# A row sum moved to VectorE, transposes made 32-bit, and three table loads moved behind a stage

## The reference, cut to what matters

```python
def reference(x, ...):                      # x: 8192 tokens x 4096 features, f32
    # layer 0a: LayerNorm, then up/gate projections, powers of |gate - point|, and a gated FFN
    a = attn_ref(layernorm(x))              # 4096 -> 1024 (x2), 7 x 1024 -> 4096, 4096 -> 9984 (x2) -> 4096
    x = x + layernorm(a)
    # layer 0b: LayerNorm, base projection plus a routed LoRA term
    xf = layernorm(x)
    base   = xf @ W_base.T + b_base         # 4096 -> 4096
    logits = xf @ W_router.T                # 8 experts, top 2
    h      = einsum('td,erd->ter', xf, A)   # 8 x 16 = 128 columns
    lora   = einsum('ter,te,eor->to', h, w, B) * 2
    return x + layernorm(base + lora)
```

## Time and profile before

| | us |
|---|---|
| timed runs | 6504.11 and 6038.73, median 6271.42 |
| the profiled execution | 6004.29 |
| its span, slowest core (core 5) | 6002.7 |
| its span, fastest core (core 3) | 5988.6 |

### The profile page before, as it was taken

One profiled execution on the slowest core, in us unless ns is written; L12 is line 12 of the kernel. 1 busy time (PEld: TensorE's weight loads), 2 busy tenths in 40 slices (PEclk: granted clock), 3 DMA queues, 4 the chain that ended last, 5 costly groups with the idle time before them and its releaser, 6 DMA issues.

```text
span 6002.7 us, 59549 instructions; the slowest of 8 cores (5988.6 to 6002.7 us)
## 1 busy us (share of the span) xinstructions
PE 5013.6 (84%) x23204; PEld 2279.0 (38%) x23204; DVE 942.9 (16%) x1384; ACT 486.2 (8%) x621; POOL 196.9 (3%) x371
## 2 busy tenths in 40 slices
PE   3887999999899999998999999799799800599940
PEld 2433444444344444443444444344344300244420
DVE  4551000011000000110000011011122233222221
ACT  3231000000000000000000000000000033100001
POOL 0000000000000000000000000000000000000000
PEclk9998999999999999999999999899899955799975
DMA  4344444445534334664343366666655733244445
GB/s 121 82 97 95 74 81 71 71 104 124 113 71 80 75 74 94 170 161 91 70 83 72 64 156 166 168 167 159 154 132 126 130 130 157 77 86 94 87 145 227
DMA packets 188163, 675.14 MB, mean 112 GB/s; under 512 B 21226, under 2 KB 86900, under 8 KB 154484
## 3 DMA queue, kind: packets, MB, share of 16 engines
q0 software_dynamic: 60784, 356.60, 33.7%
q1 hardware_dynamic: 127108, 314.73, 14.8%
HBM read 878.97 MB, written 148.90 MB: 171 GB/s over the span
## 4 chain that ended last, share of the span: by engine, by line
PE 77%; DMA 9%; DVE 7%; ACT 3%; issue 3%; SPq 1%; DVEq 0%; ACTq 0%; POOL 0%; POOLq 0%
PE P L222 74%; DMA xraw<-x_in 2%; DMA ft<-sc_f 2%; DMA W_glob<-w_fd_p 1%; ACT dt_sb L530 1%; DVE tmpr L543 1%; SPq L63 1%; PE S L239 1%; DVE tn L444 1%; DVE XL L453 1%; DMA BIG<-sc_tmp 1%; DMA W_glob<-w_fu_p 1%; DMA a1in<-sc_a1A 1%; DVE oring L1088 1%; DVE stc L813 1%
## 5 line engine op out<-in xcount | busy, mean ns | idle before, releaser
L222 PE MATMUL P<-XL,W_glob 128*128 128x512 bf16 x13056 | 2841.6, 380 | 110.6 <-DMA W_glob<-w_fu_p 42.7
L222 PE MATMUL P<-BIG,W_glob 128*128 128x512 bf16 x8576 | 1876.8, 381 | 114.5 <-DMA BIG<-sc_tmp 81.0
L222 PEld LDWEIGHTS P<-XL,W_glob 128*128 128x128 bf16 x13056 | 1274.7, 98 | 1663.9 <-issue 146.2
L222 PEld LDWEIGHTS P<-BIG,W_glob 128*128 128x128 bf16 x8576 | 835.5, 98 | 1142.0 <-issue 159.9
L599 DVE TENSOR_TENSOR BIG<-silu_sb,P 128x512 bf16<-128x512 f32 x156 | 107.3, 688 | 2105.0 <-PE P L222 2105.0
L594 ACT ACTIVATE silu_sb<-P 128x512 f32<-128x512 f32 x156 | 93.1, 597 | 2839.3 <-PE P L222 2839.3
L855 PE MATMUL P<-identb_sb,xlnb 128*128 128x128 bf16 x256 | 34.9, 304 | 294.3 <-DVE xlnb L843 285.2
L702 DVE TENSOR_TENSOR a_ring<-P,a1in 128x512 f32<-128x512 f32 x128 | 88.6, 692 | 778.3 <-PE P L222 346.3
L631 DVE TENSOR_TENSOR a1out<-P,a1in 128x512 f32<-128x512 f32 x128 | 88.6, 692 | 660.5 <-PE P L222 393.4
L713 ACT ACTIVATE sq<-a_ring 128x512 bf16<-128x512 f32 x64 | 40.4, 631 | 1314.0 <-DVE a_ring L702 1314.0
L855 PEld LDWEIGHTS P<-identb_sb,xlnb 128*128 128x128 bf16 x256 | 23.5, 132 | 305.6 <-issue 305.6
(11 more groups left out here) (124 smaller groups left out, 1213.9 us busy)
## 6 DMA issues: line engine op xcount, KB each, us to landing
W_glob<-w_fg_p POOLq DMA_DIRECT2D x78, 1024.0 KB, 9.5
W_glob<-w_fu_p POOLq DMA_DIRECT2D x78, 1024.0 KB, 13.9
W_glob<-w_fd_p POOLq DMA_DIRECT2D x96, 832.0 KB, 9.0
W_glob<-w_cat_p POOLq DMA_DIRECT2D x64, 896.0 KB, 9.1
xraw<-x_in SPq DMA_DIRECT2D x16, 2048.0 KB, 14.2
a1in<-sc_a1A SPq DMA_DIRECT2D x64, 512.0 KB, 8.3
W_glob<-w_b_p POOLq DMA_DIRECT2D x32, 1024.0 KB, 10.3
sc_a1A<-a1out SPq DMA_DIRECT2D x32, 512.0 KB, 2.7
```

The source lines that it names most:

```text
L222: inst = eng.matmul(out, l, r, start=(extra_first_start and i == 0), stop=(i == n - 1), skip_group_check=True)
```

## The change

The row sum of stage 1 moves from ScalarE to VectorE. In stage 6 xlnb6 becomes f32, and with it the transposes and their PSUM tile. The three tables are allocated after stage 6, and the first of their loads waits for the last VectorE and the last ScalarE operation of stage 6; the two others and the w_b loads stand behind it in the queue. rtm5 and rtm8 get buffers of their own.

```diff
@@ start of the program
-    asb8 = p_stack.enter_context(nc.sbuf_tensor("asb8", [128, HC * 128], BF16, side="right"))
-    wr8 = ...("wr8", [128, HC * 8], BF16) ; bfl8 = ...("bfl8", [128, D], BF16)
@@ stage 1
-        tsum = S(lambda e, b=b, o=o: e.activation(
-            junk1[:, :], xraw[:, b * D:(b + 1) * D], AF.Identity,
-            accum_out=stc[:, o + 0:o + 1]), [ld] + stc_free[b])
+        tsum = V(lambda e, b=b, o=o: e.reduce_sum(
+            stc[:, o + 0:o + 1], xraw[:, b * D:(b + 1) * D], mybir.AxisListType.X),
+            [ld])
         tsq = S(lambda e, b=b, o=o: e.activation(
             junk1[:, :], xraw[:, b * D:(b + 1) * D], AF.Square,
-            accum_out=stc[:, o + 1:o + 2]), [ld])
+            accum_out=stc[:, o + 1:o + 2]), [ld] + stc_free[b])
@@ stage 5
-    rtm5 = W_glob[:, 8192:10240].bitcast(F32)
+    rtm5 = sbr("rtm5", [128, T_CORE], F32)
@@ stage 6
-    xlnb6 = sbr("xlnb6", [128, 2048], BF16)
+    xlnb6 = sbr("xlnb6", [128, 2048], F32)
...
-                        inst = eng.transpose(pbb[:, jj * 128:(jj + 1) * 128],
+                        inst = eng.transpose(Pb[pbi][:, jj * 128:(jj + 1) * 128],
                                              xlnb6[:, c_loc * 128:
                                                    (c_loc + 1) * 128],
-                                             identb[:, :])
+                                             ident[:, :])
...
-                    dst, Pb[pbi][:, :].bitcast(BF16)[:, 0:512].rearrange(
+                    dst, Pb[pbi][:, :].rearrange(
                         "p (c t) -> p c t", c=4), AF.Copy), [tpt])
@@ head of stage 8
+    asb8, wr8, bfl8 = ... (the same shapes, allocated here)
+    ph6_done = [(s_v, s_v.n), (s_s, s_s.n)]
     P.dma("gpsimd", asb8[:, :].rearrange("p (c f) -> p c f", c=HC),
-          a_T.rearrange("(c p) f -> p c f", p=128), [], s_k2)
+          a_T.rearrange("(c p) f -> p c f", p=128), ph6_done, s_k2)
     P.dma("gpsimd", wr8..., w_rT..., [], s_k2)
     P.dma("gpsimd", bfl8[:, :], b_fl, [], s_k2)
...
-    rtm8 = W_glob[:, 8192:10240].bitcast(F32)
+    rtm8 = sbr("rtm8", [128, T_CORE], F32)
```

More of the change, by code:

```diff
@@ L349, in build_core_program @@
     p_stack = contextlib.ExitStack()
[L350 to L355, removed]
     P.dma("sync", ident[:, :], ident_d.ap(), [], s_k)
@@ L851, in tpx @@
                     inst = None
-                    pbb = Pb[pbi][:, :].bitcast(BF16)
                     for jj in range(4):
                         c_loc = (4 * g + jj) - hh * 16
-                        inst = eng.transpose(pbb[:, jj * 128:(jj + 1) * 128],
+                        inst = eng.transpose(Pb[pbi][:, jj * 128:(jj + 1) * 128],
                                              xlnb6[:, c_loc * 128:
                                                    (c_loc + 1) * 128],
-                                             identb[:, :])
+                                             ident[:, :])
                     return inst
@@ L877, in build_core_program @@
     ph_close()
+    asb8 = p_stack.enter_context(
+        nc.sbuf_tensor("asb8", [128, HC * 128], BF16, side="right"))
+    wr8 = p_stack.enter_context(
+        nc.sbuf_tensor("wr8", [128, HC * 8], BF16, side="right"))
+    bfl8 = p_stack.enter_context(
+        nc.sbuf_tensor("bfl8", [128, D], BF16, side="right"))
     ph_open()
```

## The result

The changed kernel is slower by 0.75%: the ratio to the kernel before is 1.0075, with a 95% interval of 1.0046 to 1.0104. On the 6019 to 6055 us that the kernel before takes, that is 45 us (28 to 63). The forecast was a loss of 60 us and a class "within 2%", and both held.

The account below looks back on a forecast made before the run. TensorE held 77% of the chain that ended last, and only the rest could move. Terms 28.8 + 22.4 - 8.2 - 6.7 + 23.5 gave +59.8 us: 6064 or 6099 by base, middle 6080, range 6030 to 6150.

Parts of the forecast that it names:

- the base: Time of the kernel before to which the sum was added: 6004.29 us profiled or 6038.73 us timed, not the median 6271.42.
- Stage 1: Row sum: a VectorE reduction of 4.66 us uncovered in seven tiles, less 3.8 gained in tile 0; +28.8 us.
- Stage 6, VectorE: L843 writing f32 instead of bf16 would cost nothing; other bound +13.8 us.
- Stage 6, TensorE: The 256 transposes become f32 at 1.2 GHz, uncovered: +1.40 us a half, +22.4 us for eight tiles.
- The wait of a reader: Stage 6: a group of four f32 transposes is usable for its reader 1.36 us after its start, from stage 1.
- rival (b): Stage 6: f32 transposes raise the clock, so the stage costs +5 and the sum is +42, 6064 us; chance 0.05.
- a clock above 0.50: Sign that the forecast is wrong: granted clock in stage 6 above 0.50, the 1.2 GHz level.
- End of stage 5: With the three table loads gone, two adds waiting for a1in get back 4.8 and 3.4 us; -8.2 us.
- barrier: After stage 5: without both w_b loads, the 14.64 us wait for the last sc_a store falls to 7.9; -6.7 us.
- Head of stage 8: First router matmul waits for the late tables, landing 29.7 us after issue; +23.5 us.
- (a): Head of stage 8: tables land very late, 91 us instead of 29.7, making the kernel slower by over 2%; chance 0.07.
- (c): Head of stage 8: tables land as quickly as other weights, +11 instead of +23.5, a sum of +47, 6069 us; chance 0.20.

Follow-up runs that it names:

- e11_same: The kernel before, unchanged, profiled once more on four more pairs of cores; stage 6 took 330 to 337 us.
- e7: The kernel before with the three table loads issued in stage 3, w_b loads left in place; barrier stretch 17.9 us, stage 6 328 to 332 us.
- e4: The kernel before with table loads in stage 3 and the first two w_b loads waiting for the statistics behind stage 5's barrier; ratio 0.9987.
- e6_late_split: As e3_late, but wr8 loaded first and each table with its own semaphore; head of stage 8 10.1 to 10.5 us on first cores, 15.9 to 18.1 on second.
- e3_late: The kernel before with only the table loads, and w_b behind them, waiting for the end of stage 6; ratio 1.0003 (0.9977 to 1.0029).
- e8_pre6: The kernel before with stage 6's loads of the next tile queued ahead of the tile's store; 5912.05 us against 6010 to 6043.

## Why the prediction was right or wrong

**The step that failed is the last one of the sum, the base.** "I predict the middle, 6080" puts +59.8 on 6004 and 6039, two single executions, while the median shown for the kernel before was 6271.42. Set against that median 6080 reads as 3% faster, where the sum says slower. The runs showed 6049.92 as the median of 18 executions of the kernel before and 6142.57 for the changed one, and a ratio of 1.0075. The sum on 6049.92 is 6110, and 6142.57 is still in the range. A change should have been stated as a ratio first, 1.010.

**The sum** was right in its sign and near in size: +59.8 forecast, +63.6 between the medians of the profiles' cores, +45 (28 to 63) by timing. Its agreement with the profiles is in part luck, since the profile before has a stage 6 that is 10 us short. The terms as measured with least beside them are 28.8 for stage 1, 15.3 for stage 6, -8 and -10.5 for the end of stage 5 and 20.5 for the head of stage 8: 46, which the timing bears out.

**Stage 1** (+28.8): right step by step; measured alone too.

**Stage 6, VectorE** (0): right. L837 takes 1.35 us.

**Stage 6, TensorE** (+22.4): the serial mechanism was right, and this is the mis-sized term of the sum; measured +15.3 without load waits, and +17 from e11_same to the changed kernel (333.4 to 350.1; +26.2 in the table is against the short draw). Two steps of it fail. The wait of a reader was taken from VectorE in stage 1, 1.36 us, where ScalarE starts 1.24 us after the group (4867.33 to 4868.57), and that enters twice: 1.18 for a half instead of 1.40, 18.7 to 18.9 in all. The rest is the clock: rival (b) came true in part, given a chance of 0.05, and its sign did (0.53, and the forecast named a clock above 0.50 as a sign of being wrong). I had quoted the Trainium skill (TensorE: Matmul & The Clock Gate, Part 4: PE-mode transpose), that transposes do not count as activity that frees the clock; the stretch at 0.93 with transposes alone speaks against it, so here the measurement decides.

**End of stage 5** (-8.2) and **barrier** (-6.7): the mechanisms were right, and e7 and e4 tell their causes apart. The barrier term was too small, -10.5: I took the median landing of a store to sc_a, 7.9 us, which itself has loads beside it; alone the wait is 3.67. The first term measured -5 between these two profiles, within their spread. All profiles give it back: with the tables at this place stages 2 to 5 take 4581.9 to 4589.4 us (medians of five profiles), without them 4574.3 to 4584.1 (eight), and the middles are 8 us apart. So -8.2 stands, though two adds of one core were thin ground for it.

**Head of stage 8** (+23.5): +20.5 as a median, but +16.5 on first and +24.8 on second cores of a pair (forecast of one kind for all), and the slower kind decides. In it 3.2 us between the last eviction and the issue of the first load were missed, though a row showed 2.53 of them. The rivals (a) and (c) didn't come.

**What the prediction lacked altogether** is the pair. It reasoned on one core. The late tables drive a pair apart, from 11 to 12 us at the start of stage 9 (10 to 11 in e11_same) to 16 to 18, because the second core waits 8 us longer; at 18.4, pair 6/7 of the changed kernel, stage 9 took 242 and 245 us. Its 242 us, 11 more than the 231 of core 0, the next slowest, are what put core 6 9 us behind it. That the distance makes stage 9 long is read from the table and not shown by an edit.

## What to carry to other kernels

A stage that is a serial chain of load, work and store hands every microsecond of an edit to the end; here the order of one queue was worth 110 us, the edit in question 15. When a load is moved off a place, read what waited there for the queue behind it too: the gain sat at a barrier. And before a difference of 10 us between two profiles is explained, profile the same kernel again and compare core by core: what the other core of a pair moved during the loads changed a stage by as much.

## What the runs showed of the hardware

- TensorE's granted clock rose to 0.93 in a stretch of 3 us in which TensorE ran only f32 transposes (changed kernel, core 6); in the same stage with bf16 transposes it stayed at 0.50.
- A VectorE operation with two column operands over 2048 f32 columns took 1.35 us with bf16 and with f32 output alike.
- The first strided load on the GpSimd queue was issued 3.2 us after the end of the eviction that released it (changed kernel, core 6, and e6_late_split, core 2).
- Three loads of 1024, 64 and 1024 KB (SBUF side) on one queue (e3_late): the last is there 20 us after the first issue on the first core of a pair and 27 on the second, which issues some 9 us later; wr8 (64 KB) took 6.5 us when first (e6_late_split) and 10.3 when second.
- The loads of a tile in stage 6 took 16.6 us while the other core of the pair moved nothing and 18.8 while it moved 3.2 to 3.9 MB. With 2 x 1024 KB of weights issued in the same moment, those of the first tile took 20.1 to 24.3 us (e4_early_hold) instead of 12.6 to 14.4.
- A core moved 248 GB/s over 160 us in e8_pre6 while its partner moved 236, and 222 in stage 9 of the kernel before, where the serial order was the limit.
